# Two graph layers with residual norms in one kernel: Strassen products for the tiles used by both layers

## The reference

```python
x_drop = x * (u >= 0.1) / (1.0 - 0.1)
h = layernorm(x + adj @ x_drop)                    # first layer
out = layernorm(h + adj @ (h @ weight) + bias)     # second layer
# layernorm: over the 64 features, eps 1e-5, no gain
```

## Time and profile before

| | us |
|---|---|
| median of 3 runs (lowest to highest) | 957.52 (956.88 to 958.76) |
| profiled execution, its own time | 957.39 |
| its span, first to last instruction | 955.6 |
| PE busy | 914.3 (96%) |
| DVE busy | 211.0 (22%) |
| ACT, POOL busy | 29.9, 24.1 (3% each) |
| DMA | 359.37 MB, 334 tile loads of 1 MB and 39 smaller transfers, 376 GB/s mean |
| granted TensorE clock, mean | 0.989 of full speed |

### The profile page before, as it was taken

How to read it: one execution, slowest core, us unless ns; L and a number is a source line. 1 busy time by engine, 2 the same in 40 slices (tenths; PEclk the granted TensorE clock), 3 DMA queues, 4 the chain that set the end, 5 groups by cost and what they waited for, 6 DMA issues and landing times.

```text
span 955.6 us, 9830 instructions
## 1 busy us (share of the span) xinstructions
PE 914.3 (96%) x4288; PEld 307.9 (32%) x4288; DVE 211.0 (22%) x431; ACT 29.9 (3%) x68; POOL 24.1 (3%) x23
## 2 busy tenths in 40 slices
PE   5679999999999999999999999999999999999795
PEld 1123333333333333333333333333333333333242
DVE  1111121131131221212213111312131211220378
ACT  0010000000000000000000000000000000000011
POOL 2000000000000000000000000000000000000123
PEclk9899999999999999999999999999999999999998
DMA  9999999999979899799999999998989999999901
GB/s 347 404 419 421 421 421 419 420 380 422 392 305 422 334 378 417 315 413 378 358 421 386 418 371 415 374 419 330 421 317 423 364 404 421 414 422 421 417 32 67
DMA packets 57340, 359.37 MB, mean 376 GB/s; under 512 B 6353, under 2 KB 14545, under 8 KB 14545
## 3 DMA queue, kind: packets, MB, share of 16 engines
q1 hardware_dynamic: 57296, 358.74, 92.3%
HBM read 356.61 MB, written 2.10 MB: 375 GB/s over the span
## 4 chain that ended last, share of the span: by engine, by line
PE 88%; DMA 5%; DVE 4%; SPq 3%; issue 1%; ACT 0%; DVEq 0%
PE psum L569 26%; PE psum L574 21%; PE psum L614 19%; PE psum L598 17%; DMA tiles<-adj_t 5%; PE psum L620 3%; SPq L330 2%; PE psum L635 1%; DVE sums L415 1%; DVE vsum L422 1%; DVE layer L516 1%; SPq L309 0%; DVE layer L458 0%; PE psum L579 0%; DVE layer L416 0%
## 5 line engine op out<-in xcount | busy, mean ns | idle before, releaser
L574 PE MATMUL psum<-tiles,stat 128*64 128x512 f32 x548 | 253.7, 612 | 24.1 <-DMA tiles<-adj_t 24.1
L569 PE MATMUL psum<-tiles,stat 128*64 128x512 f32 x1136 | 253.8, 593 | 0.0
L579 PE MATMUL psum<-tiles,stat 128*64 128x512 f32 x548 | 253.7, 612 | 0.0
L614 PE MATMUL psum<-tiles,stat 128*64 128x512 f32 x944 | 212.4, 596 | 5.6 <-DVE stat L510 5.6
L458 DVE TENSOR_TENSOR layer<-psum,layer 128x512 f32<-128x512 f32 (+1 forms) x126 | 87.0, 690 | 479.7 <-PE psum L614 232.2
L598 PE MATMUL psum<-tiles,stat 128*64 128x512 f32 x768 | 169.1, 593 | 0.0
L574 PEld LDWEIGHTS psum<-tiles,stat 128*64 128x64 f32 x548 | 75.6, 141 | 191.0 <-issue 149.6
L569 PEld LDWEIGHTS psum<-tiles,stat 128*64 128x64 f32 x1136 | 80.7, 137 | 158.1 <-issue 158.1
L614 PEld LDWEIGHTS psum<-tiles,stat 128*64 128x64 f32 x944 | 67.8, 138 | 138.1 <-issue 137.4
L598 PEld LDWEIGHTS psum<-tiles,stat 128*64 128x64 f32 x768 | 54.8, 137 | 108.0 <-issue 108.0
L579 PEld LDWEIGHTS psum<-tiles,stat 128*64 128x64 f32 x548 | 75.6, 141 | 0.0
(11 more groups left out here) (36 smaller groups left out, 152.1 us busy)
## 6 DMA issues: line engine op xcount, KB each, us to landing
tiles<-adj_t SPq DMA_DIRECT2D x334, 1024.0 KB, 11.6
x_res<-x SPq DMA_DIRECT2D x16, 128.0 KB, 10.5
out<-layer SPq DMA_DIRECT2D x8, 256.0 KB, 2.1
tiles<-u SPq DMA_DIRECT2D x3, 512.0 KB, 14.1
tiles<-x SPq DMA_DIRECT2D x3, 512.0 KB, 15.1
tiles<-u SPq DMA_DIRECT2D x1, 384.0 KB, 6.3
tiles<-x SPq DMA_DIRECT2D x1, 384.0 KB, 6.9
tiles<-u SPq DMA_DIRECT2D x1, 128.0 KB, 2.1
```

The lines of the kernel that those rows point to most:

```text
L569: last = pe.matmul(sum_a[i % 2][to, :], stat[:, j * C + c, half], tile[:, c], start=begun.get(("a", to.start)) != i, stop=False, skip_grou ...
L574: last = pe.matmul(sum_a[i % 2][low, :], stat[:, j * C + c, 0:D], tile[:, c], start=begun.get(("a", 0)) != i, stop=ends and c == 2, skip_g ...
L579: last = pe.matmul(sum_b[i % 2][high, :], stat[:, j * C + c, 0:D], tile[:, c], start=begun.get(("b", D)) != i, stop=ends and c == 3, skip_ ...
L614: last = pe.matmul(bank[to, :], stat[:, j * C + c, D:2 * D], tile[:, c], start=c == 0, stop=c == C - 1)
```

## The change

A fused job multiplies the tile's four chunks by two stationary sides, x and h. Seen as a 2 x 2 block product (chunks 0, 1 and 2, 3; left and right half of the 512 columns; x and h), that is 8 products of half size; the new form makes 7, on sums of tile blocks and on sums of x and h blocks. DVE makes the sums (`operands`), PE adds up the seven products of all fused jobs of a row in two PSUM banks, and DVE combines them once a row (`combine`: nine instructions on 64 partitions x 256 elements, then two additions of 512). A quarter of the job (4 of its 14 matmuls, all of 256 columns) needs no sums and goes ahead of the wait for them. With this go:
- the sums take two buffers in SBUF (20 KB a partition), and SLOTS falls from 17 to 14;
- EARLY falls from 4 to 2: columns 0 and 1 are early jobs, rows from 3 on have fused jobs with columns 2 to i - 1;
- the planner reckons a fused job as 19 in place of 22, and places the reloads of the last row and the jobs around turn 15 otherwise;
- h is scaled by the mean over partitions of the largest |x_drop|, which DVE takes by two reductions of x_drop for each group in the start; the last layernorm's eps is scaled with it;
- `weight` and `bias` are centred over the output features in turn 14 (five small DVE instructions, `centre_weights`), and the two instructions that centred the rows in each final (L415, L416) are gone;
- the first layer's sums of `first` jobs now have both halves in one bank.

```diff
-SLOTS = 17
-EARLY = 4
+SLOTS = 14
+EARLY = 2
+AHEAD = 3
...
-WORK_OF_HALF = 11
+WORK = {"first": 11, "second": 11, "fused": 19, "pair": 22, "early": 44}
...
+LAST_KEPT = 5
...
+        summed = len(heavy) == 0
...
-            elif len(again) > AGAIN_KEPT:
+            elif len(again) > (LAST_KEPT if i == NB - 1 else AGAIN_KEPT):
                 chosen = again
+            elif i == NB - 1:
+                chosen = light or heavy or early
             else:
                 chosen = light or again or (early if due else heavy)
             put(chosen.pop(0))
+            if not summed and not heavy:
+                jobs.append(("combine", i))
+                summed = True
         for job in near:
             put(job)
...
-    jobs += again[:2]
+    jobs += again[:1]
     jobs.append(("turn", NB - 1))
-    jobs += again[2:]
+    jobs += again[1:]
...
+    fused_jobs = [job for job in jobs if job[0] == "fused"]
+    tile_jobs = [job for job in jobs if job[0] in TILE_JOBS]
+    latest_freed, freed_for = 0, {}
+    for load in loads:
+        latest_freed = max(latest_freed, load[4])
+        freed_for[load[0:2], load[5]] = latest_freed
+
+
+    sums_from = []
+    for n, job in enumerate(fused_jobs):
+        begin = max(tile_jobs.index(job) - AHEAD, freed_for[job[1:3], "fused"])
+        if n >= 2:
+            begin = max(begin, tile_jobs.index(fused_jobs[n - 2]) + 1)
+        sums_from.append(begin)
...
+            def operands(n):
+
+                _, i, j = fused_jobs[n]
+                if n >= 2:
+                    dve.wait_ge(tile_jobs_done, done_after[fused_jobs[n - 2]])
+                dve.wait_ge(h_ready, j + 1)
+                t = stat_sums[:, n % 2]
+                columns = stat[:, j * C:(j + 1) * C]
+                x_j, h_j = columns[:, :, 0:D], columns[:, :, D:2 * D]
+                step(dve.tensor_tensor(out=t[:, 0], in0=h_j[:, 0:2], in1=x_j[:, 0:2], op=ALU.subtract))
+                dve.tensor_tensor(out=t[:, 1], in0=h_j[:, 2:4], in1=h_j[:, 0:2], op=ALU.subtract).then_inc(dve_step, 1)
+                step(dve.tensor_tensor(out=t[:, 2], in0=h_j[:, 2:4], in1=t[:, 0], op=ALU.subtract), 2)
+                step(dve.tensor_tensor(out=t[:, 3], in0=t[:, 2], in1=x_j[:, 2:4], op=ALU.subtract))
+                slot, use = place[fused_jobs[n], (i, j)]
+                dve.wait_ge(s_arrived[slot], 16 * (use + 1))
+                tile, a = tiles[:, slot], tile_sums[:, n % 2]
+                step(dve.tensor_tensor(out=a[:, 0:2], in0=tile[:, 0:2].rearrange("p k (v m) -> p v k m", v=2),
+                                       in1=tile[:, :, B // 2:B].rearrange("p (v k) m -> p v k m", v=2), op=ALU.add))
+                step(dve.tensor_tensor(out=a[:, 2], in0=a[:, 1], in1=tile[:, 0:2, 0:B // 2], op=ALU.add))
+                dve.tensor_tensor(out=a[:, 3], in0=tile[:, 2:4, 0:B // 2], in1=a[:, 2],
+                                  op=ALU.add).then_inc(operands_ready, 1)
+
+            def combine(i):
+
+                low, high = slice(0, D), slice(D, P)
+                left, right = slice(0, B // 2), slice(B // 2, B)
+                t_0, t_1 = [work[0:D, n].rearrange("p c d -> p (c d)") for n in range(2)]
+                t_2 = third[:, :]
+                side = of_row(i)
+
+                def minus(out, product, addend, op1=ALU.add):
+
+                    return dve.scalar_tensor_tensor(out=out, in0=product, scalar=-1.0, in1=addend, op0=ALU.mult, op1=op1)
+
+                step(dve.tensor_copy(t_0, products[0][low, left]))
+                dve.tensor_tensor(out=row_sums[side, 0, left], in0=products[0][high, left], in1=t_0,
+                                  op=ALU.add).then_inc(dve_step, 1)
...
+                dve.scalar_tensor_tensor(out=row_sums[side, 0, right], in0=products[1][low, right], scalar=-1.0,
+                                         in1=t_2, op0=ALU.mult, op1=ALU.add).then_inc(combined, 1)
+                dve.tensor_tensor(out=row_sums[side, 1, right], in0=products[1][high, left], in1=t_2,
+                                  op=ALU.add).then_inc(combined, 1)
+
...
             for job in jobs:
-                if job[0] == "early":
+                while n_operands < len(fused_jobs) and sums_from[n_operands] <= n_tile_jobs:
+                    operands(n_operands)
+                    n_operands += 1
+                if job[0] in TILE_JOBS:
+                    n_tile_jobs += 1
+                if job[0] == "combine":
+                    i = job[1]
+                    dve.wait_ge(tile_jobs_done, done_after[job])
+                    combine(i)
+                    n_combined += 1
+                    dve.wait_ge(combined, 2 * n_combined)
+                    dve.wait_ge(added, n_second)
+                    side = of_row(i)
+                    step(dve.tensor_tensor(out=layer1_pair(i)[side, :], in0=layer1_pair(i)[side, :],
+                                           in1=row_sums[side, 0], op=ALU.add))
+                    dve.tensor_tensor(out=layer2_block(i), in0=layer2_block(i), in1=row_sums[side, 1],
+                                      op=ALU.add).then_inc(own_joined, 1)
...
                         dve.wait_ge(added, n_second)
-                        source = sum_b if i % 2 else sum_a
-                        dve.tensor_tensor(out=halves[of_row(i), :], in0=source[i % 2][of_row(i), :],
+                        dve.tensor_tensor(out=halves[of_row(i), :], in0=sum_f[i % 2][of_row(i), :],
                                           in1=layer1_pair(i)[of_row(i), :], op=ALU.add).then_inc(half_by_dve, 1)
-                        if has_fused(i):
-                            dve.tensor_tensor(out=layer2_block(i), in0=sum_a[i % 2][D:P, :], in1=layer2_block(i),
-                                              op=ALU.add).then_inc(layer2_summed, 1)
...
-                    dve.tensor_tensor(out=stat[:, i * C:(i + 1) * C, D:2 * D], in0=r[:, :, :],
-                                      in1=over_features(rstd[:, 0, 0:C]), op=ALU.mult).then_inc(h_ready, 1)
+                    dve.scalar_tensor_tensor(out=stat[:, i * C:(i + 1) * C, D:2 * D], in0=r[:, :, :], scalar=scale[:, 0:1],
+                                             in1=over_features(rstd[:, 0, 0:C]), op0=ALU.mult,
+                                             op1=ALU.mult).then_inc(h_ready, 1)
...
-                    dve.wait_ge(product_read, n + 1)
-                    centre(output_rows(n), 2 * C)
+                    norms += 1
                     if n:
                         pair_inverse_root(n - 1).then_inc(rstd_ready, 1)
-                    variance(output_squares, var[:, n % 2], 2 * C)
+                    variance(output_squares, var[:, n % 2], 2 * C, scale[:, 1:2])
...
-                    for c in range(C):
-                        if kind == "fused":
-                            for to, half in (low, slice(0, D)), (high, slice(D, 2 * D)):
-                                last = pe.matmul(sum_a[i % 2][to, :], stat[:, j * C + c, half], tile[:, c],
-                                                 start=begun.get(("a", to.start)) != i, stop=False,
-                                                 skip_group_check=True)
...
+                    else:
+                        new = begun.get("products") != i
+                        begun["products"] = i
+                        if new:
+                            pe.wait_ge(combined, 2 * combined_rows(i - 1))
+                        if j + 1 > h_seen:
+                            pe.wait_ge(h_ready, j + 1)
+                            h_seen = j + 1
+                        n = fused_jobs.index(job)
+                        left, right = slice(0, B // 2), slice(B // 2, B)
+                        a, t = tile_sums[:, n % 2], stat_sums[:, n % 2]
+
+
+                        for k in range(2):
+                            pe.matmul(products[0][low, left], stat[:, j * C + k, 0:D], tile[:, k, left],
+                                      start=new and k == 0, stop=False, skip_group_check=True)
+                            pe.matmul(products[0][high, left], stat[:, j * C + 2 + k, 0:D], tile[:, 2 + k, left],
+                                      start=new and k == 0, stop=False, skip_group_check=True)
+                        pe.wait_ge(operands_ready, n + 1)
+                        pe.matmul(products[0][low, right], t[:, 1, 0], a[:, 0, 0],
+                                  start=False, stop=False, skip_group_check=True)
+                        pe.matmul(products[0][high, right], t[:, 1, 1], a[:, 0, 1],
+                                  start=False, stop=False, skip_group_check=True)
+                        for k in range(2):
+                            pe.matmul(products[1][low, left], t[:, 2, k], a[:, 2, k],
+                                      start=new and k == 0, stop=False, skip_group_check=True)
+                            pe.matmul(products[1][high, left], t[:, 0, k], a[:, 1, k],
```

(40 more changed lines are left out.)

126 lines of the change are left out of this document (80 added, 46 removed).

## The result

| | us | ratio to before (95% interval) |
|---|---|---|
| before | 957.21 (956.88 to 958.76) | |
| after | 998.12 (992.65 to 999.55) | 1.0408 (1.0389 to 1.0426) |

Slower by 41 us, where 27 were forecast; the profiled execution has a span of 996.5 for the 982.4 of the sum.

A forecast was written before the change was run, and what follows sets the result against it. Bound: PE's work plus a start and an end. 955.6 - 37.5 - 5.6 - 2.8 + 3.9 + 35.8 (turns 4-11) + 24.5 (turns 12-15) + 7 + 1.5 = 982.4 us span, 984 us measured time; range 955 to 1000.

The forecast's parts named there:

- Sign and place: At changes of row, DVE's stream costs more than PE's 37.5 us saving: 984 us, chance of slower 0.80.
- Slots, early columns, start, order of the end, centring: Outside the rows: start 3.9 us longer with 14 slots; at the end 5.6 (wait for h) and 2.8 (centring) saved.
- DVE's order with tiles in time: Turns 4 to 11: if tiles come early, DVE's order alone loses 17.5 us.
- rival A: At changes of row, tiles are there in time and only DVE's order costs: 966 us, chance 0.18.
- Arrival of the tiles: Turns 4 to 11: sums also wait for tiles from a queue of loads, so 35.8 us are lost instead of 17.5.
- What a late tile costs: Change of row: loss a + 6.5 us, a being tile landing relative to the first fused job's start; row 9: 4.8.
- Runs of fused jobs: Inside rows: PE outpaces DVE's sums, losing 0.5 us per run of three, 1.5 per four; 7 in all.
- The clock: After PE's waits: lower clock mostly falls on jobs DVE's chain covers; only the 7.1 us stall pays, 1.5 us.
- Turns 12 to 14: Late rows: PE waits for sums, combination, row_end and h, losing 6.7, 5.4 and 10.7 us.
- The end: Last row: the 5.6 us wait for h goes, centring saves 2.8, turn 15 loses 1.65.
- Rival B: DVE at changes of row: sums always ready, 915 us without stalls; faster has chance 0.15, mostly 930 to 955.

The follow-up runs named there:

- e3_old_job: The changed kernel with the old fused job of eight 512-column matmuls, no operand sums and no nine combining instructions: 953.25 us.
- f4_before_tail: The kernel before with only the order of the last row and around turn 15 changed: 949.89 us.
- e2_no_arrival: The changed kernel with DVE's tile-side sums reading the other sums buffer from the second job on, so DVE never waits for a load: 967.36 us.
- e4_dummies: The changed kernel with unused matmuls filling PE's waits ahead of the transposes and of the fused job's sums: 993.52 us.
- f1_split: The changed kernel with the four small stationary-side sums of each fused job moved from DVE to POOL: 977.02 us.
- g2_hybrid2: The changed kernel with the first two fused jobs of a row plain and the other 66 using seven products: 992.94 us.

## Why the prediction was right, and where its size was off

- **Sign and place: right.** PE's saving is real and is not what sets the time; DVE's stream at the change of row is. Without sums 925.72, with all of them 998.12.
- **Slots, early columns, start, order of the end, centring: right.** Their terms give 955.6 - 5.6 - 2.8 + 3.9 + 1.8 = 952.9; e3_old_job took 953.25. One term is off by itself: the order of the end pays about 8 in f4_before_tail for 5.6, and e3_old_job loses 3.3 in its rows, which the terms do not have.
- **DVE's order with tiles in time: right.** The rival A had 966 for it; e2_no_arrival took 967.36.
- **Arrival of the tiles: the term that was too small.** The difference between forecast and rival A was 18.3 us; between the two runs it is 30.8, which is 12.5 of the 14.1 by which the sum was short. By rows, the 18.3 were forecast for rows 5 to 12 (turns 4 to 11), where 28.1 were lost, and row 4, put at nothing, lost 1.8. The step put eleven loads behind P(4,7): the smallest time from issue to landing for the first, 2.49 for each of the others, 30.2 us in all. In the trace P(4,7) ends at 440.97 (437.54 + 3.43), F(9,2) starts 31.93 later (31.9 forecast), and its tile is there after at most 31.6. The stretches of after:

```profile
440.60:472.60 32.00, 31.73 (x192) 14.95 (x190) 20.21 (x41) 0.00 (x0) 0.00 (x0) 1.00 0.99 408
444.00:472.60 28.60, 28.33 (x176) 13.60 (x174) 18.51 (x36) 0.00 (x0) 0.00 (x0) 1.00 1.01 422
```

  32.00 us at 408 GB/s are 13.1 MB, where eleven loads and an x_res block are 11.7. So 1.4 MB of other loads went over in the same time. One load issued earlier (at 437.60) was still under way, which is 1.05 MB at most; the rest, 0.3 MB or more, belongs to loads issued behind that of F(9,2), since several are under way at once and share the rate. The first of the eleven took 5.2 us from issue to landing, not the 4.7 of the earlier trace rows, at which in before at most one other load was under way. In the same way, counted from when PE was done with the row before (PE itself waits for the tile up to 0.9 us of it), DVE's sums of the row's first fused job start at 1.1, 0.9, -1.4, -0.3, 1.0 and -0.2 us in turns 5 to 10, for forecasts of -1.1, -0.9, -3.0, -1.7, -1.7 and -2.0: on average 1.9 later.
- **What a late tile costs: right.** The rule was a + 6.5 a row. With a = -0.3 row 9 lost 5.7, with 1.1 and 0.9 rows 6 and 7 lost 7.3 and 6.7, with -1.4 row 8 lost 5.3, with 1.0 row 10 lost 7.5: a + 5.8 to 6.7. Row 11 (a = -0.2) lost 9.7, but 3.6 of that are a run of fused jobs further on (see the runs). The sums of a fused job follow each other at a pitch of 3.77 (472.60 to 476.37) for the 4.02 reckoned, since DVE begins an instruction that does not need the one before it up to 0.08 before that ends (475.20, where L554 ends at 475.28).
- **Runs of fused jobs: right in sum, not in place.** Reckoned were 0.5 us for each run of three, 1.5 for one of four, 7 in all. PE waits for sums inside a row only at F(11,7) (1.92), F(13,7) (1.93) and F(14,12) (0.52), and the lower clock behind each of the first two costs 1.7 more: 7.8.
- **The clock: its place right, its size open.** 1.5 reckoned; filling the waits brought back 4.6 for 13.6 us of clock (e4_dummies), while 5.1 us of clock were still missing. Waits of 2.2 us are followed by records at half pace in some rows [the stretch at 429.40, 0.57], which I had only seen after 3.55 us. That most of it falls on jobs that DVE's chain covers, as the prediction said, is why h's waits are 11.4 us and not some 2 in each of ten rows. The Trainium skill ("TensorE: Matmul & The Clock Gate", section "HAM oscillation — how this bites in real kernels") describes such a kernel, whose waits between groups of matmuls drop the clock again each time. The trace agrees on the drop (0.57) and not on each time (1.00 at 536.20, after a wait of 2.21), and e4_dummies says that here it costs little.
- **Turns 12 to 14: near.** 22.8 were forecast, and with the 4.0 for the runs and the 1.5 for the clock in these rows it is 28.3; rows 13 to 15 lost 30.1. The tiles' arrival has no part in it, since e2_no_arrival loses 30.4 there. The wait for the combination was 6.0 for 7.1.
- **The end: 2.2 better than reckoned.** PE's work behind row_end 15 is 20.6 us longer (six pairs of 3.43 more stand there) while its length grew by 11.6, a gain of 9.0 for 5.6 + 2.8 - 1.65 = 6.8. The 2.4 by which the order pays more than its term in f4_before_tail are of this size. Further 1.9 were small losses of rows 4 to 15 before that the sum kept. With 18.3 more lost in the rows than the 67.1 forecast, this makes 18.3 - 2.2 - 1.9 = 14.2, which is the miss.
- **Rival B's 915 could not have been reached:** with no sums at all it is 925.72, and rows 4 to 15 still lose 11.7, in part to loads. Of PE's 37.5 us at most 27.5 were to be had (953.25 - 925.72).

What stays open: why the clock falls behind some waits and not behind others of the same length, what the order of the end gains beyond its wait, how the tiles' arrival adds up at changes of row other than the one worked out, and how far POOL's and DVE's accesses explain f1_split.

## What to carry to other kernels

When work is moved from the bounding engine to an idle one, look at the idle engine's order at the narrowest place and not at its share: 59% busy hid a queue of three jobs' sums in front of the one instruction that everybody waited for. A wait for a load in front of it comes on top (30.8 us of the 72 here), and is easily left out of the sum: g2_hybrid2 missed its forecast by 45 us mainly through it. Use the cheaper form only where the helper has slack: in the same plan 45 jobs gave 12 us over none (941.4 for 953.3), all 91 cost 45. And price a load's arrival in a full queue by all the bytes that go over until it lands, those of the loads before and behind it too, not by the smallest time ever seen.

## What the hardware showed that was not expected

- Two 64-column matmul chains side by side keep pace at 256 columns: starts 0.216 apart with weight loads of 0.14 each.
- After a wait of 2.21 us PE ran 4 us at a granted clock of 0.57 in one row (429.40), and after one of 2.21 at 1.00 in another (536.20).
- DVE's 512-element sums went from 692 to 766 ns and its 1024-element ones from 1225 to 1259 while POOL made small sums at 605 to 792 ns each.
